# Attention scores as three float32r products in two 64-row halves of the array, in place of six bf16 products over 96 rows

## The chip, the cores and the metric

The kernel runs on one core of a Trainium2 chip. The metric is the device time of one execution in microseconds (us). Engines: PE (TensorE, matmuls), DVE (VectorE), ACT (ScalarE), POOL (GpSimd), SP (SyncE, which issues most DMAs). PEld is PE's weight load.

## What is computed

```python
xn = layernorm(x)                               # x: [4, 2048, 256] float32
q, k, v = xn @ wq.T, xn @ wk.T, xn @ wv.T       # 16 heads of 16; 4 groups share a k and a v head
att = softmax(causal(q k^T / 4)); attn = (att v) @ wo.T
# soft mixture of 16 experts with 64 slots each
y = layernorm(xn) * norm_g + norm_b
logits = y . layernorm(slot_embeds); dispatch = softmax over tokens; combine = softmax over slots
slots = dispatch^T y; eout = (gelu(slots Wg + bg) * (slots Wu + bu)) Wd + bd
out = x + attn + combine eout
```

All is computed to about float32 accuracy, so products are made of parts: a float32 number is split into several numbers of a narrower type, and the products of the parts are summed.

## The kernel before

The stages run one after another, each a block with an instruction stream per engine and semaphores between them: prepare, project, attend, dispatch, experts, combine.

`project` goes over 16 chunks of 512 tokens. DVE takes layer-norm statistics (L303, L306) and normalises x and then xn (L319, giving xn and y), POOL makes the reciprocal roots (L351, L353), PE transposes and makes q, k and v (L450; `pj` has three PSUM banks of q, q and v|k), ACT copies. q and k are split into three bf16 parts: ACT casts `pj` to part 0 (L407), DVE subtracts it to `rest` (L327), ACT casts `rest` to part 1 (L413), POOL subtracts to part 2 (L361, `thirds`). SP writes the parts, y, y transposed and v to DRAM.

`attend` works per batch (4) and group (4): `qs` holds the parts of q stacked in 6 x 16 = 96 rows, `ks` those of k, in the orders `Q_PART` and `K_PART`, so that one matmul over 96 rows sums six products of parts. Two more rows (97 and 98) hold minus the row maximum (`mrow`, as two bf16 parts) in `qs` and ones in `ks`. A group has 40 units: (c, kb) are 512 queries and 128 keys. In a step PE makes

- four s products (L768) of the unit into `sT`, for four heads, in two pairs, each pair followed by an exp on ACT (L642, 128 x 1024), which POOL masks on the diagonal (L624);
- four x products (L726): the same scores the other way around, for 128 queries and up to 512 keys, 20 steps ahead (`LEAD`), into three PSUM banks `mb` (`NBANK`). DVE takes their maxima, with L666 below the diagonal and the masked L671 of 128 to 512 columns on it. `MAXES` gives their order;
- the V product (L751) of the step before: four heads into four 32-column strips of the array, plain float32, eight instructions.

`entries` puts the x products in the step: one after each pair of s, one or more after, V, and one last. At the end of each c DVE makes nm and nml (L701 to L706), PE transposes (L731), DVE copies to `mrow` (L685), and SP writes the row to `qs` (L601). The context goes out by L737, L690, L693 and L604. Twenty steps of x alone lead in (250 to 300 us in the trace). `load(b, g)` on SP fetches a group (13 DMAs, L585 to L587); the four first loads come at the start, later ones when a group is done. PE is one in-order stream: the code lets it wait for DVE's bank, for ACT's exp and for the loads in turn.

Of the kernel before, what the change touches and what calls it, by code (L numbers as in the profile page):

```python
# [23 lines left out]
P = 128  # L24
# [16 lines left out]
Q_PART = (0, 0, 1, 1, 0, 2)  # L41
K_PART = (0, 1, 0, 1, 2, 0)
KR = HD * len(Q_PART)
VW = 32
# [26 lines left out]
def prepare(nc, w, io):  # L71
    with ExitStack() as ctx:
# [12 lines left out]
        ident, identb = w["ident"], w["identb"]  # L85
# [20 lines left out]
        with nc.Block() as block:  # L106
# [21 lines left out]
            def _(pool):  # L128
# [7 lines left out]
                pool.wait_ge(zeroed, 3)  # L136
# [3 lines left out]
                pool.wait_ge(made, 1)  # L140
                nc.gpsimd.tensor_copy(identb[:], ident[:]).then_inc(made, 1)
                pool.wait_ge(step, 2 * SB)
                nc.gpsimd.tensor_scalar(rs[:], mv[:, :, 1], EPS, None, ALU.add).then_inc(made, 1)
                pool.wait_ge(made, 4)
# [3 lines left out]
            def _(dve):  # L148
# [27 lines left out]
                for i, (parts, dest, _) in enumerate(jobs):  # L176
                    dve.wait_ge(turned, i + 1)
                    src = bank[:, i % 8, 0:dest.shape[1]]
                    if i == 0:
                        for k in range(DK):  # L180
                            ins = nc.vector.tensor_copy(
                                w["wqT"][:, k, :].rearrange("p (g d h) -> p g h d", g=NKV, h=GS),
                                bank[:, 0, k * D:(k + 1) * D].rearrange("p (g h d) -> p g h d", g=NKV, h=GS))
# [11 lines left out]
            def _(pe):  # L195
                pe.wait_ge(made, 3)
# [12 lines left out]
def project(nc, w, io, scr):  # L209

    with ExitStack() as ctx:
# [9 lines left out]
        part = a.sb("part", [P, 2, 3, 3, CH], BF16)  # L221
        rest = a.sb("rest", [P, 3, CH])
# [14 lines left out]
        pj_ready, p1_ready, rest_ready, p2_ready, p3_ready = (  # L237
            sem(n) for n in ("pj_ready", "p1_ready", "rest_ready", "p2_ready", "p3_ready"))
# [4 lines left out]
        credits = [(xn_ready, 2 * TPC), (xT_kept, DK), (yT_kept, DK), (rest_ready, 3),  # L243
                   (p3_ready, 3), (v_ready, 1), (vp_ready, 1), (out[0], 16 * NOUT), (out[1], 16 * NOUT),
# [16 lines left out]
        with nc.Block() as block:  # L261
            @block.sync
            def _(sp):
# [5 lines left out]
                def chunk(i, j, q):  # L269
                    sp.wait_ge(y_ready, i * TPC + TPC)  # L270
                    sp.dma_start(scr["y"][i], y[:, q]).then_inc(out[q], 16)
                    wait_apart(sp, p3_ready, 3 * i + 6, passed)
                    for m in range(2):
                        sp.dma_start(scr["q_out"][i, m], part[:, q, m]).then_inc(out[q], 16)
                    sp.dma_start(scr["k_out"][i], part[64:128, q, 2]).then_inc(out[q], 16)
# [12 lines left out]
            def _(dve):  # L288
# [186 lines left out]
def attend(nc, w, scr):  # L475
# [19 lines left out]
    with ExitStack() as ctx:  # L495
# [80 lines left out]
        with nc.Block() as block:  # L576
            @block.sync
            def _(sp):
# [11 lines left out]
                for g in range(NKV):  # L590
                    load(0, g)
# [899 lines left out]
```

## Time and profile before

| | |
|---|---|
| median of 3 runs | 3144.43 us (3142.61 to 3147.72) |
| profiled execution, span from first to last instruction | 3140.2 us |
| profiled execution's own time outside its span | not shown |
| PE / PEld / DVE / ACT / POOL busy | 2696.9 / 1453.6 / 2430.9 / 1627.3 / 622.6 us |
| granted TensorE clock, mean | 0.946 of 2.4 GHz |

A group of instructions is given by line, engine, operation, `out<-in`, and shape as partitions x elements. "Idle before" names what ended the wait. Busy time counts overlapping instructions once, and a matmul's length has its latency in it: the pace of a stream is read from starts.

### The profile page before, as it was taken

The numbers are of one execution on the slowest core, as the hardware profiler recorded it, in microseconds if no ns is written. First come the engines' busy times: TensorE is split into PE (matmuls) and PEld (weight loads), VectorE is DVE, ScalarE is ACT, GpSimd is POOL, SyncE is SP. The second block draws the span as 40 slices with busy tenths as digits, with TensorE's granted clock in tenths as the row PEclk, the third lists the DMA queues.
The fourth block names the chain that finished last, engine by engine and source line by source line (L and its number), as shares of the span: only waits on it lengthen the run. The fifth ranks groups of instructions, "written<-read, shape, count | busy, mean of one in ns | idle before, by whom it ended". The sixth has DMA issues, their size and how long they took to land. (4 is left out here: it accounts for less than half of the span.)

```text
span 3140.2 us, 58475 instructions
## 1 busy us (share of the span) xinstructions
PE 2696.9 (86%) x17059; PEld 1453.6 (46%) x17059; DVE 2430.9 (77%) x5354; ACT 1627.3 (52%) x2185; POOL 622.6 (20%) x574
## 2 busy tenths in 40 slices
PE   4766999998999998999999999985776866879999
PEld 2431333332333332333333333345675756879999
DVE  6976888887888887888888888747677875755666
ACT  2650666665666665666666666665555652112222
POOL 2540011010010000001000000145254533532000
PEclk8985999998999998999999999998998988989999
DMA  3778022022022202202202000031413314656564
GB/s 121 248 240 106 7 35 35 5 36 34 5 37 35 26 15 35 29 11 35 35 14 28 6 7 5 8 124 66 161 29 145 107 54 154 196 164 221 192 194 151
DMA packets 191631, 247.75 MB, mean 79 GB/s; under 512 B 69892, under 2 KB 146824, under 8 KB 191400
## 3 DMA queue, kind: packets, MB, share of 16 engines
q1 hardware_dynamic: 170632, 224.99, 28.2%
q10 hardware_dynamic: 20768, 19.93, 1.9%
q8 instruction: 115, 1.88, 0.3%
q14 instruction: 116, 0.95, 0.1%
HBM read 148.87 MB, written 95.45 MB: 78 GB/s over the span
## 5 line engine op out<-in xcount | busy, mean ns | idle before, releaser
L642 ACT ACTIVATE att_pr<-att_sT 128x1024 f32<-128x1024 f32 (+3 forms) x1280 | 1080.8, 895 | 709.4 <-PE att_sT L768 708.5
L666 DVE TENSOR_REDUCE att_mx<-att_mb 128x1 f32<-128x512 f32 x1536 | 1000.6, 686 | 65.6 <-PE att_mb L726 44.9
L726 PE MATMUL att_mb<-att_ks,att_qs 96*128 96x512 bf16 (+3 forms) x2560 | 831.3, 360 | 68.7 <-DMA att_v<-v_rows 33.7
L768 PE MATMUL att_sT<-att_qs,att_ks 98*128 98x512 bf16 (+3 forms) x2560 | 680.6, 350 | 22.5 <-issue 11.4
L671 DVE CUSTOM_DVE_ANT_0 att_junk<-att_mb,w_causal 128x128 bf16<-128x128 f32 (+3 forms) x1024 | 491.6, 488 | 187.6 <-PE att_mb L726 131.8
L726 PEld LDWEIGHTS att_mb<-att_ks,att_qs 96*128 96x128 bf16 x2560 | 248.1, 97 | 777.6 <-DVE att_mx L666 318.5
L751 PE MATMUL att_acc<-att_pr,att_v 128*32 128x512 f32 (+3 forms) x5120 | 604.3, 544 | 3.8 <-POOL att_pr L624 1.8
L624 POOL TENSOR_SCALAR_AFFINE_SELECT att_pr<-att_pr 128x512 f32<-128x512 f32 x256 | 162.4, 635 | 1681.8 <-ACT att_pr L642 1681.8
L768 PEld LDWEIGHTS att_sT<-att_qs,att_ks 98*128 98x128 bf16 x2560 | 244.7, 99 | 212.2 <-issue 29.1
L1310 ACT CAST com_e1h<-com_tp 128x1024 fp32r<-128x1024 f32 x64 | 64.5, 1014 | 262.6 <-PE com_tp L1383 236.4
L928 DVE TENSOR_TENSOR dis_dl<-dis_lg,dis_dh 128x512 fp32r<-128x512 f32 x128 | 149.8, 1193 | 59.5 <-ACT dis_dh L894 58.6
L751 PEld LDWEIGHTS att_acc<-att_pr,att_v 128*32 128x32 f32 x5120 | 102.3, 108 | 183.2 <-issue 165.9
L1036 PE MATMUL dis_lp<-dis_yh,dis_dh 128*128 128x258 f32 x256 | 78.2, 306 | 106.6 <-DVE dis_dl L928 106.6
L1401 PE MATMUL com_mp<-com_eoh,com_e1h 128*128 x512 | 146.3, 286 | 7.9 <-DVE com_e1l L1335 7.9
L1401 PE MATMUL com_mp<-com_eol,com_e1h 128*128 x512 | 145.9, 285 | 0.0
L1401 PE MATMUL com_mp<-com_eoh,com_e1l 128*128 x512 | 145.8, 285 | 0.0
L894 ACT CAST dis_dh<-dis_lg 128x512 fp32r<-128x512 f32 x128 | 79.0, 617 | 89.6 <-PE dis_dp L1036 49.4
L888 ACT ACTIVATE dis_lg<-dis_lg 128x512 f32<-128x512 f32 x128 | 79.8, 627 | 70.8 <-POOL dis_lg L996 70.8
L1011 PE MATMUL dis_lp<-w_seTh,dis_yTh 128*128 128x512 f32 x256 | 102.3, 400 | 12.6 <-POOL dis_yTl L977 11.7
L996 POOL TENSOR_TENSOR dis_lg<-dis_lg,dis_ca 128x512 f32<-128x512 f32 x64 | 100.2, 1598 | 56.9 <-issue 56.9
L1036 PEld LDWEIGHTS dis_lp<-dis_yh,dis_dh 128*128 128x128 f32 x256 | 51.6, 202 | 112.0 <-DVE dis_dl L928 112.0
L1401 PEld LDWEIGHTS com_mp<-com_eoh,com_e1h 128*128 128x128 f32 x512 | 99.3, 194 | 8.7 <-issue 8.7
(170 smaller groups left out, 4051.4 us busy)
## 6 DMA issues: line engine op xcount, KB each, us to landing
slot_exps<-dis_e SPq DMA_DIRECT2D x64, 512.0 KB, 2.7
com_e<-slot_exps SPq DMA_DIRECT2D x64, 512.0 KB, 3.5
att_qs<-q_parts SPq DMA_DIRECT2D x96, 256.0 KB, 9.7
q_parts<-proj_part SPq DMA_DIRECT2D x32, 384.0 KB, 3.3
y_rows<-proj_y SPq DMA_DIRECT2D x16, 512.0 KB, 4.6
y_cols<-proj_yT SPq DMA_DIRECT2D x16, 512.0 KB, 4.6
context<-att_cn SPq DMA_DIRECT2D x64, 128.0 KB, 2.0
dis_yT<-y_cols SPq DMA_DIRECT2D x16, 512.0 KB, 3.5
```

The lines of the kernel that those rows point to most:

```text
L624: nc.gpsimd.affine_select(out=blk, in_=blk, compare_op=ALU.is_ge, fill=0.0, base=0, pattern=[[0, GS], [1, P]], channel_multiplier=-1).then ...
L642: nc.scalar.activation(pr[:, s % 4, 2 * hf:2 * hf + 2, off:CH], sT[:, 2 * hf:2 * hf + 2, off:CH], ACT.Exp, scale=float(HD) ** -0.5).then_i ...
L666: nc.vector.tensor_reduce(dst, mb[:, bank, :], AX.X, ALU.max).then_inc(mb_used, 1)
L671: nc.vector.tensor_tensor_reduce(junk[:, t % 2, 0:wd], mb[:, bank, 0:wd], w["causal"][:, CH - wd:CH], 1.0, LOW, ALU.add, ALU.max, dst).the ...
L726: last = nc.tensor.matmul(mb[:, bank, 0:wd], qs[0:KR, g % NKV, c, q0:q0 + P], ks[0:KR, g % NKV, j * CH:j * CH + wd], start=True, stop=True)
L751: last = nc.tensor.matmul(acc[VW * h:VW * (h + 1), off:CH], v[:, g, kb, :], pr[:, s % 4, h, off:CH], start=(kb == 0), stop=(kb == TPC * (c ...
L768: last = nc.tensor.matmul(sT[:, h, off:CH], ks[:, g, kb * P:(kb + 1) * P], qs[:, g, c, h * CH + off:(h + 1) * CH], start=True, stop=True)
L928: nc.vector.tensor_tensor(dl[:, m % ND], lg[:, t, hf * 512:(hf + 1) * 512], dh[:, m % ND].bitcast(F32), ALU.subtract).then_inc(dl_ready, 1)
L996: nc.gpsimd.tensor_tensor(lg[:, t, h], lg[:, t, h], ca[:, h], ALU.subtract).then_inc(sub_p, 1)
L1011: last = nc.tensor.matmul(lp[:, 2 * (t % 2) + h, :], lhs[:, t // TPC, k, (t % TPC) * P:(t % TPC + 1) * P], w[rhs][:, k, h * 512:(h + 1) * ...
L1036: last = nc.tensor.matmul(bank(hf * HB + s)[:, 0:D + 2], lhs[:, (hf * TPB + t) % ND, s * P:(s + 1) * P], rhs[:, t, :], start=(t == 0 and l ...
L1401: last = nc.tensor.matmul(mp[:, q, 0:D], lhs[:, q, s, :], rhs[:, b, s, :], start=(s == 0 and rhs is eoh and lhs is e1h), stop=(s == SB - 1 ...
```

## The change

q and k are split into two float32r parts (no second cast on ACT, no thirds on POOL, no `rest`), and three products of parts are summed: 48 rows in place of 96. `qs` and `ks` are float32r and hold two copies side by side: rows 0 to 49 for two of the four heads, rows 64 to 113 for the other two (k is loaded twice). The x and s products of one head then use only the upper or lower 64 rows of the array. The order of `MAXES` has the head innermost, so that successive x products alternate the halves; within a step all four x now have the same t and j. The rows of ones come by DMA, and PE waits for them first. V, ACT's exps, the kinds and number of DVE's maxima and all later stages are as before.

```diff
-Q_PART = (0, 0, 1, 1, 0, 2)
-K_PART = (0, 1, 0, 1, 2, 0)
+Q_PART = (0, 0, 1)
+K_PART = (0, 1, 0)
 KR = HD * len(Q_PART)
+RG = 64
+NRG = P // RG
+HL = GS // NRG
...
-        part = a.sb("part", [P, 2, 3, 3, CH], BF16)
-        rest = a.sb("rest", [P, 3, CH])
+        part = a.sb("part", [P, 2, 3, 2, CH], F32R)
...
                 def splits(i, q):
                     for s in range(3):
-                        dve.wait_ge(p1_ready, 3 * i + s + 1)
-                        dve.wait_ge(p3_ready, 3 * i + s + 1)
+                        dve.wait_ge(high_ready, 3 * i + s + 1)
                         r = rows(s)
-                        nc.vector.tensor_tensor(rest[r, s, :], pj[r, s, :], part[r, q, s, 0, :],
-                                                ALU.subtract).then_inc(rest_ready, 1)
+                        nc.vector.tensor_tensor(part[r, q, s, 1, :], pj[r, s, :], part[r, q, s, 0, :].bitcast(F32),
+                                                ALU.subtract).then_inc(low_ready, 1)
...
-                def thirds(i, q):
-                    for s in range(3):
-                        pool.wait_ge(p2_ready, 3 * i + s + 1)
-                        pool.wait_ge(p3_ready, 3 * i + s + 3)
-                        r = rows(s)
-                        nc.gpsimd.tensor_tensor(part[r, q, s, 2, :], rest[r, s, :], part[r, q, s, 1, :],
-                                                ALU.subtract).then_inc(p3_ready, 1)
...
-                    for s in range(3):
-                        r = rows(s)
-                        act.wait_ge(rest_ready, 3 * i + 3 + s + 1)
-                        nc.scalar.copy(part[r, q, s, 1, :], rest[r, s, :]).then_inc(p2_ready, 1)
...
-    MAXES = [(c, h, t, j) for c in range(CPB) for h in range(GS) for t in range(TPC) for j in range(c + 1)]
+    MAXES = [(c, h, t, j) for c in range(CPB) for t in range(TPC) for j in range(c + 1) for h in range(GS)]
...
-        qs = a.sb("qs", [KR + 2, NKV, CPB, GS * CH], BF16)
-        ks = a.sb("ks", [KR + 2, NKV, S], BF16)
+        qs = a.sb("qs", [RG + KR + 2, NKV, CPB, HL * CH], F32R)
+        ks = a.sb("ks", [RG + KR + 2, NKV, S], F32R)
...
                 def load(b, g):
-                    for j in range(len(Q_PART)):
-                        r = slice(HD * j, HD * (j + 1))
-                        sp.dma_start(qs[r, g], scr["q_in"][b, Q_PART[j], g]).then_inc(loaded[g], 16)
-                        sp.dma_start(ks[r, g], scr["k_in"][b, K_PART[j], g]).then_inc(loaded[g], 16)
+                    for rg in range(NRG):
+                        for j in range(len(Q_PART)):
+                            r = slice(RG * rg + HD * j, RG * rg + HD * (j + 1))
+                            sp.dma_start(qs[r, g].bitcast(F32), scr["q_in"][b, Q_PART[j], g, rg]).then_inc(loaded[g], 16)
+                            sp.dma_start(ks[r, g].bitcast(F32), scr["k_in"][b, K_PART[j], g]).then_inc(loaded[g], 16)
...
-                for g in range(NKV):
+                load(0, 0)
+                for rg in range(NRG):
+                    for hl in range(2):
+                        row = RG * rg + KR + hl
+                        sp.dma_start(ks[row:row + 1].rearrange("o g s -> o (g s)").bitcast(F32),
+                                     w["ones"][:].bitcast(F32)).then_inc(ones_set, 16)
+                for g in range(1, NKV):
                     load(0, g)
...
-                nc.vector.memset(ks[KR:KR + 2, :, :], 1.0).then_inc(ones_set, 1)
...
-                            for hl in range(2):
-                                sp.dma_start(qs[KR + hl:KR + hl + 1, g % NKV, c, :],
-                                             mrow[hl * ROWS:(hl + 1) * ROWS, c, :]).then_inc(m_rows[c], 16)
+                            for rg in range(NRG):
+                                row = RG * rg + KR
+                                sp.dma_start(qs[row:row + 2, g % NKV, c, :].bitcast(F32),
+                                             mrow[rg * ROWS:(rg + 1) * ROWS, c, :].bitcast(F32)).then_inc(m_rows[c], 16)
...
-                            q0 = h * CH + t * P
+                            r = slice(RG * (h % NRG), RG * (h % NRG) + KR)
+                            q0 = h // NRG * CH + t * P
                             wd = CH if j < c else (t + 1) * P
-                            last = nc.tensor.matmul(mb[:, bank, 0:wd], qs[0:KR, g % NKV, c, q0:q0 + P],
-                                                    ks[0:KR, g % NKV, j * CH:j * CH + wd], start=True, stop=True)
+                            last = nc.tensor.matmul(mb[:, bank, 0:wd], qs[r, g % NKV, c, q0:q0 + P],
+                                                    ks[r, g % NKV, j * CH:j * CH + wd], start=True, stop=True)
...
-                            for h in (2 * hf, 2 * hf + 1):
-                                last = nc.tensor.matmul(sT[:, h, off:CH], ks[:, g, kb * P:(kb + 1) * P],
-                                                        qs[:, g, c, h * CH + off:(h + 1) * CH], start=True, stop=True)
+                            for rg in ((0, 1), (1, 0))[hf]:
+                                r = slice(RG * rg, RG * rg + KR + 2)
+                                last = nc.tensor.matmul(sT[:, NRG * hf + rg, off:CH], ks[r, g, kb * P:(kb + 1) * P],
+                                                        qs[r, g, c, hf * CH + off:(hf + 1) * CH], start=True, stop=True)
```

`q_out` and `k_out` write two float32 parts in place of three bf16 ones; nml and mrow are float32r (32 x 128 float32 is transposed and copied), in an order by halves; the four copies of wq transposed in prepare put the heads by halves.

## Rows read from the trace of the kernel before

**Rows 1.** The page's first line

```profile
span 3140.2 us, 58475 instructions
```

**Rows 2.** Windows: stretch, length, busy us (instructions) by engine, clock, DMA share, GB/s

```profile
120.00:150.00 30.00, 23.34 (x93) 13.34 (x94) 28.64 (x72) 18.50 (x33) 18.02 (x21) 0.94 0.83 267
250.00:300.00 50.00, 36.97 (x82) 8.52 (x82) 42.01 (x130) 0.00 (x0) 0.00 (x0) 0.50 1.07 128
524.30:633.30 109.00, 103.43 (x662) 35.49 (x661) 94.84 (x250) 69.27 (x85) 10.15 (x16) 1.00 0.20 27
```

**Rows 3.** Groups by shape, DVE, one group of attention (866.4 to 975.3)

```profile
L693 DVE TENSOR_TENSOR att_cn<-att_mb,att_rz 128x256 f32<-128x256 f32 x4 | 1.7, 424 | 0.2
L690 DVE RECIPROCAL att_rz<-att_mb 128x16 f32<-128x16 f32 x4 | 1.0, 258 | 0.3 <-DVE att_mx L666 0.2
L685 DVE COPY att_mrow<-att_mb 32x128 bf16<-32x128 bf16 x4 | 0.8, 204 | 0.0
```

**Rows 4.** Timeline of PE, one step: start us, length us, what

```profile
1006.73 0.23 PE L726 MATMUL att_mb<-att_ks,att_qs 96*128 96x128 bf16 x1
...
1007.90 0.60 PE L726 MATMUL att_mb<-att_ks,att_qs 96*128 96x512 bf16 x2
1008.43 1.07 PE L751 MATMUL att_acc<-att_pr,att_v 128*32 128x512 f32 x8
1009.43 0.28 PE L726 MATMUL att_mb<-att_ks,att_qs 96*128 96x256 bf16 x1
```

**Rows 5.** Timeline of DVE in attention, masked and full maxima

```profile
922.49 0.29 DVE L671 CUSTOM_DVE_ANT_0 att_junk<-att_mb,w_causal 128x128 bf16<-128x128 f32 x1
...
922.78 0.42 DVE L671 CUSTOM_DVE_ANT_0 att_junk<-att_mb,w_causal 128x256 bf16<-128x256 f32 x1
...
923.14 0.56 DVE L671 CUSTOM_DVE_ANT_0 att_junk<-att_mb,w_causal 128x384 bf16<-128x384 f32 x1
...
1005.29 0.68 DVE L671 CUSTOM_DVE_ANT_0 att_junk<-att_mb,w_causal 128x512 bf16<-128x512 f32 x1
...
1005.90 1.88 DVE L666 TENSOR_REDUCE att_mx<-att_mb 128x1 f32<-128x512 f32 x3
1007.70 0.28 DVE L671 CUSTOM_DVE_ANT_0 att_junk<-att_mb,w_causal 128x128 bf16<-128x128 f32 x1
```

**Rows 6.** Timelines of PE, dispatch and combine: float32r products back to back

```profile
2250.42 0.39 PE L1011 MATMUL dis_lp<-w_seTl,dis_yTh 128*128 128x512 f32 x1
2250.65 0.40 PE L1011 MATMUL dis_lp<-w_seTh,dis_yTl 128*128 128x512 f32 x1
...
2900.05 0.19 PEld L1401 LDWEIGHTS com_mp<-com_eol,com_e1h 128*128 128x128 f32 x1
2900.17 0.19 PEld L1401 LDWEIGHTS com_mp<-com_eoh,com_e1l 128*128 128x128 f32 x1
```

**Rows 7.** Timelines in projection: PE, POOL, DVE and SP

```profile
122.10 0.65 SPq L271 DMA_DIRECT2D y_rows<-proj_y  x1
...
124.94 3.62 POOL L361 TENSOR_TENSOR proj_part<-proj_rest,proj_part 128x512 bf16<-128x512 f32 x3
...
125.48 3.56 DVE L319 TENSOR_SCALAR proj_y<-proj_xn,proj_mv,proj_rs 128x256 f32<-128x256 f32 x4
...
130.87 1.38 DVE L319 TENSOR_SCALAR proj_xn<-proj_x,proj_mv,proj_rs 128x256 f32<-128x256 f32 x4
...
139.76 1.88 PE L450 MATMUL proj_pj<-proj_xT,w_wkvT 128*128 128x512 f32 x4
...
144.00 0.65 SPq L271 DMA_DIRECT2D y_rows<-proj_y  x1
```

**Rows 8.** Loads: PE's and SP's timelines

```profile
301.82 0.61 PE L768 MATMUL att_sT<-att_qs,att_ks 98*128 98x512 bf16 x1 [8.68 <-DMA att_qs<-att_mrow]
...
415.52 0.38 SPq L585 DMA_DIRECT2D att_qs<-q_parts  x1
...
421.82 0.39 SPq L587 DMA_DIRECT2D att_v<-v_rows  x1
```

More of the change, by code:

```diff
@@ L135, in _ @@
                 nc.gpsimd.memset(w["causal"][:], 0.0).then_inc(zeroed, 1)
-                pool.wait_ge(zeroed, 3)
+                nc.gpsimd.memset(w["ones"][:].bitcast(F32), 1.0).then_inc(zeroed, 1)
+                pool.wait_ge(zeroed, 4)
                 tri = w["causal"][:, CH - P:CH]
@@ L180, in _ @@
                         for k in range(DK):
-                            ins = nc.vector.tensor_copy(
-                                w["wqT"][:, k, :].rearrange("p (g d h) -> p g h d", g=NKV, h=GS),
-                                bank[:, 0, k * D:(k + 1) * D].rearrange("p (g h d) -> p g h d", g=NKV, h=GS))
+                            for r in range(NRG):
+                                ins = nc.vector.tensor_copy(
+                                    w["wqT"][:, k, :].rearrange("p (g d r e) -> p r g e d", g=NKV, d=HD, r=NRG)[:, r],
+                                    bank[:, 0, k * D:(k + 1) * D].rearrange("p (g e r d) -> p r g e d", g=NKV, r=NRG,
+                                                                            d=HD)[:, r])
                         ins.then_inc(kept, 1)
@@ L271, in chunk @@
                     sp.dma_start(scr["y"][i], y[:, q]).then_inc(out[q], 16)
[L272 removed]
+                    wait_apart(sp, low_ready, 3 * i + 6, passed)
                     for m in range(2):
[L274 to L275 removed]
+                        sp.dma_start(scr["q_out"][i, m], part[:, q, m].bitcast(F32)).then_inc(out[q], 16)
+                    sp.dma_start(scr["k_out"][i], part[64:128, q, 2].bitcast(F32)).then_inc(out[q], 16)
                     sp.wait_ge(yT_kept, DK * i + 2 * DK)
@@ L369, in step @@
                         roots(1, i + 1, 1 - q)
-                    thirds(i, q)
                 roots(0, 0, 0)
@@ L504, in attend @@
         nm = a.sb("nm", [P, ROWS])
-        nml = a.sb("nml", [P, 2, ROWS], BF16)
-        mrow = a.sb("mrow", [2 * ROWS, CPB, P], BF16)
+        nml = a.sb("nml", [P, NRG, 2, HL * TPC], F32R)
+        mrow = a.sb("mrow", [2 * ROWS, CPB, P], F32R)
         cT = a.sb("cT", [P, 2, CH])
@@ L730, in fill @@
                             pe.wait_ge(nm_ready, b * NMC + g * CPB + c + 1)
-                            last = nc.tensor.transpose(mb[0:2 * ROWS, bank, 0:P // 2].bitcast(BF16),
-                                                       nml[:, :, :].rearrange("p a r -> p (a r)"), w["identb"][:])
+                            last = nc.tensor.transpose(mb[0:2 * ROWS, bank, 0:P],
+                                                       nml[:].rearrange("p r a x -> p (r a x)").bitcast(F32),
+                                                       w["ident"][:])
                         else:
```

46 lines of the change are left out of this document (21 added, 25 removed).

## The prediction

> **What bounds the kernel now.** I read the page first, then windows by stage, then the groups of one steady stretch, and last timelines of single steps. The windows split the 3140.2 us span [rows 1]: weights and projection until 230, a lead-in of row maxima from 250 to 300, attention from 301.8 to about 2068, and then dispatch, experts and combine, which the change does not touch. Attention is 56% of the span and repeats every 109 us, one group of 40 steps (4 batches x 4 groups = 16 groups). In such a group PE is busy 103.4 us and DVE 94.8 [rows 2].
>
> A step holds four score products for the maxima (x, L726), four transposed score products (s, L768), eight value matmuls (V, L751) and, on DVE, four maxima. The starts on PE in one full step [rows 4] show what paces it: from 1006.73 (a 128-wide x) through 4 s and 3 x of 512 columns to the V at 1008.43 is 1.70 us, and from there to the next x at 1009.43 is 1.00. A bf16 product of 512 columns thus takes 0.22 us, and a full step 8 x 0.216 + 1.00 = 2.73 us, which is 109/40. DVE needs 0.60 us per full maximum by its starts (1005.90 to 1007.70 is three [rows 5]), 2.40 per full step. So in attention PE is the bound and DVE is close behind. ACT, 69 us per group, is not near.
>
> The lead-in is DVE and DMA: it begins when the first load has landed (250.5) and PE's first s waits until 301.8 for a DMA [rows 8], behind the loads of all four groups, at 128 GB/s with the DMA engines full [rows 2]. Projection repeats every 10.9 us (y_rows issued at 122.10 and, two chunks on, at 144.00 [rows 7]) with DVE busy 95% and DMA share 0.83 at 267 GB/s [rows 2].
>
> **The change, part by part.**
>
> *Score products, PE.* K falls from 96 or 98 rows to 48 or 50, placed in rows 0-63 or 64-127 of the array; the order of x and s now alternates the halves (0 and 1): s0 s1, x0 of half 0, s1 s0, x1 of half 1, x2 of half 0, V, x3 of half 1. If two halves run at once, a pair takes the time of one. A float32r product of 512 columns starts every 0.233 us (2250.42 to 2250.65) and one of 256 every 0.12 [rows 6], so a pair should take 0.233, or 0.117 each; the weight load of 0.188 us is seen to hide at a pitch of 0.12 in the 256-column rows. I take 0.12 each whatever the width: 8 x 0.12 = 0.96, and a full step on PE becomes 1.96 us in place of 2.73. No row shows two row halves at work. The nearest is V: four heads in four column strips, 8 matmuls in 1.00 us [rows 4], where plain float32 instructions of 512 columns over the whole array start every 0.43 us (four in 1.88, the last one's 0.59 taken off), 3.4 for eight [rows 7]. Strips do run at once there. Bounds: 0.117 per product (full overlap) and 0.233 (none). I take overlap. The Trainium skill ("TensorE: Matmul & The Clock Gate", Part 3) says that matmuls in different row groups run concurrently, four of 32 rows giving 3.07x; by that two halves would give at least 1.5x. No run here shows it yet. The skill's "TensorEngine Tiling", Key Properties, speaks against: changing the tiling mode drains the engine. Both kernels change mode twice a step around V, and the trace has about 0.1 us there (1007.90 + 2 x 0.22 = 1008.33, V at 1008.43), which is in my 1.00 and stays.
>
> *Who is the bound then.* DVE. Its maxima keep their kinds and number: per group 96 full at 0.60 and 16 each of the masked ones of 512, 384, 256 and 128 columns at 0.61, some 0.48 (between its neighbours), 0.36 and 0.29 (starts 1005.29 to .90, 922.78 to 923.14, 922.49 to .78 [rows 5]). The new order of MAXES puts four of one kind in a step: 24 steps of 4 x 0.60 = 2.40, 4 of 2.44, and 12 whose DVE work (1.92, 1.44, 1.16) is under PE's 1.96, so PE sets those. Sum of the larger: 57.6 + 9.8 + 23.5 = 90.9; nm, nml, mrow, rz and cn on DVE add 4 x (0.8 + 0.7) = 6 (0.42 for cn, four small ones of some 0.2 for nm, nml and mrow, one of 0.26 for rz [rows 3]). That is 97. Frictions: x2 must wait for its bank (three banks), then V sits in front of x3. A waiting x issues at 0.03, a float32r product lands some 0.5 later, V begins at 0.45, x3 issues at 1.45 and lands at 1.95, where DVE wants it at 1.80: 0.15 x 24 = 3.6. Group: 100.5, against 108.9. Bounds: 96.5 (no friction), and 105 if the frictions stay what they are now (PE's own work sums to 97 per group: 139,264 columns at 2.4 per ns are 58, V 35, transposes and gaps 4; the larger of PE and DVE step by step to 102; measured 109, so 6.7), with 128-wide float32r products slower than I assume. 301.8 to the last maximum is 15.5 groups: 15.5 x 8.4 = **130 us** gained (60 to 190). The last 20 steps have no maxima; ACT (1.94 per full step) and V pace them: 0. The instruction fetch between batches: unchanged.
>
> *Row of maxima.* nml, the transpose and mrow go to float32r: 4 each per group, 0.2 us each, the DMA of each half is 512 B per piece in place of 256: 0. The memset on DVE (6.88 us, in an idle stretch) is replaced by four 32 KB DMAs into single rows; PE's first instruction now waits for them behind load 0. Their 131 KB would take 1 us at the 128 GB/s of the loads; in 256-byte pieces into one row each I take 4, bounds 1 and 10.
>
> *Loads.* Each group's load goes from 13 to 25 DMAs, 0.47 us of SP each (415.52 to 421.82 is 12 steps; 11.7 us, was 6) [rows 8], and from 2.23 to 2.62 MB (q 1.57 MB either way, k 0.39 to 0.79). At 128 GB/s the four first loads take 82 us in place of 70: **+12**, and +4 for the ones. In mid-run a load takes 17 to 20 us at that rate, then 20 to 23. What queues behind it on SP and the rings is the row of maxima for c=2, issued 11.6 us after the load begins; it is due when step 12 of the group starts, 12 x 2.5 = 30 us. It would land at about 25: hidden, with 5 us to spare. Nothing else on SP is due before.
>
> *Projection.* Gone: ACT's second cast (3 x 0.62 per chunk), POOL's thirds (3.62). DVE's subtraction stays and writes the low part. The gain comes from elsewhere: DVE's four norms of y take 3.56 us while POOL runs the thirds, and the same form on x takes 1.38 when POOL is idle [rows 7]. With POOL quiet DVE's chunk is 10.9 - 2.2 = 8.7 us. The Trainium skill ("SBUF — State Buffer", the shared port pair of DVE and GpSimd, held for a whole instruction) gives the reason; the trace agrees, 0.89 against 0.35 us. But DMA grows: q_out 384 to 512 KB, k 192 to 256, 2752 to 3072 KB a chunk, 3.15 MB at 267/0.83 = 322 GB/s full rate = 9.8 us; the fastest window shows more, so 9.5. Gain 1.4 x 15 = 21, taken as **20 us**, plus 2 at the tail; bounds 0 and 33.
>
> So the first s moves from 301.8 by -22 + 12 + 4 = -6 us (-25 to +12). Sum: -130 - 6 = -136. The span is 3140.2 and the median of the runs 3144.4, the 4 us between them I leave; 3144.4 - 136 = **3008 us**.
>
> **Rivals.**
> 1. *The halves don't overlap.* Then each product costs 0.233 in place of 0.216, narrow ones 0.12 in place of 0.06: 5.4 + about 1 us per group on PE, which remains the bound, and the full/masked bunching on DVE (3.1 us steps beside short PE steps) adds 2. For: no row shows halves. Against: the column strips of V. 15.5 x 6 to 8 = +93 to 125, less 6: about **3240**, slower. The point from which it decides is a pitch of about 0.18 us per product: 8 x 0.18 + 1.0 = 2.44 is DVE's step; above 0.21 the kernel is slower.
> 2. *Overlap, but the step is held near its old length* by the chain x2-V-x3 and three banks, or by narrow products: group 105 to 109, time **3060 to 3140**. For: DVE idles 14 us per group now, most on x of PE. Against: PE would have 20% slack that it has not now.
> 3. *The clock.* PE is granted 2.4 GHz in attention (1.00), but 0.50, its 1.2 GHz level, throughout the lead-in, where it is busy 37 of 50 us, and 0.94 in projection at 23.3 of 30 [rows 2]. After the change PE idles a fifth of the step. At the low level a full step costs 1.7 + 2.0 = 3.7 us, 1.3 over DVE's. If an eighth of the 1560 us falls low, that is about 70 us back: **3080**. Against: the gaps would be under 0.5 us, where projection has gaps of 3 us and keeps 0.94.
> 4. *The load is late*: if a load takes over 29 us, the c=2 row stalls s in each of 12 groups; 5 us each, +60, **3070**. The rate of the first loads speaks against.
>
> **How the numbers follow.** Mine 0.60 (own range 2955 to 3080), rival 1 0.18, rival 2 0.10, rival 3 0.08, rival 4 0.04. The last three lie mostly between 3060 and 3135. The range is 2950 to 3130, which leaves out rival 1 and little more. The bound of what a measurement tells from no change is 0.2%, 6 us. Faster 0.79, same 0.02, slower 0.19.
>
> **What would show it.** In the profile after: s and x starts in pairs a few ns apart or 0.12 us apart on average, and not 0.23; loads of a group issued every 101 us, not 109; DVE busy over 92% of a group and PE under 85%; DVE's y norms at 0.35 us; first s near 296. A PE step of over 2.7 us with x and s at 0.23 makes rival 1 right, a granted clock under 0.95 in attention rival 3, a wait of s for mrow at kb = 0 rival 4.

## The result and the profile after

The changed kernel takes 3294.06 us (median of 4 runs, 3275.83 to 3306.62), the kernel before 3143.56 (3142.61 to 3147.72): ratio 1.0468, interval 1.0435 to 1.0501. It is slower by 150 us, where 136 us of gain were predicted. The profiled execution takes 3285.96 us. Now and then an execution of a kernel is slower at a lower clock; the ratios below leave these out. The first line of the page of the kernel after, and its windows (columns as in [rows 2]):

```profile
span 3284.2 us, 58210 instructions
```

```profile
120.00:150.00 30.00, 25.99 (x100) 14.87 (x99) 24.89 (x81) 15.52 (x29) 7.76 (x12) 0.94 0.93 318
250.00:300.00 50.00, 32.83 (x63) 17.07 (x63) 34.12 (x92) 0.00 (x0) 0.00 (x0) 0.50 1.05 127
340.00:1900.00 1560.00, 1439.95 (x8563) 627.63 (x8564) 1222.09 (x3220) 899.10 (x1090) 131.96 (x208) 0.85 0.20 26
1000.00:1120.00 120.00, 112.71 (x656) 49.41 (x653) 94.15 (x246) 68.61 (x84) 10.15 (x16) 0.82 0.22 28
1188.00:1192.00 4.00, 3.92 (x30) 1.69 (x23) 3.45 (x10) 2.46 (x4) 0.00 (x0) 1.00 0.00 0
1192.00:1196.00 4.00, 2.78 (x21) 1.43 (x18) 2.53 (x15) 2.12 (x3) 0.63 (x1) 0.90 0.01 2
1196.00:1200.00 4.00, 4.00 (x20) 1.59 (x17) 2.18 (x11) 2.23 (x4) 0.63 (x1) 0.50 0.01 2
1204.00:1208.00 4.00, 3.48 (x17) 1.54 (x9) 2.97 (x11) 1.94 (x2) 0.00 (x0) 0.50 0.00 0
1212.00:1216.00 4.00, 4.00 (x20) 2.27 (x20) 2.42 (x6) 1.94 (x2) 0.00 (x0) 0.50 0.01 2
1220.00:1224.00 4.00, 3.97 (x28) 1.61 (x23) 3.10 (x9) 3.00 (x4) 0.00 (x0) 1.00 0.02 4
```

The same window of the kernel before:

```profile
340.00:1900.00 1560.00, 1461.78 (x9256) 499.67 (x9248) 1332.13 (x3477) 972.79 (x1179) 142.13 (x224) 0.99 0.17 24
```

Attention is where the time went: the last s product starts at 2204.4 us, where it was 2063.8. The granted clock of the window from 340 to 1900 was 0.99, and is 0.85 now. Cut into windows of 5 us, 23% of that stretch are below 0.60, most of them at 0.50, the 1.2 GHz level. The last six rows follow one such episode: the clock is 1.00; PE is then busy for only 2.78 of 4 us; the clock falls, and at 1220 it is back. In between PE is busy nearly all the time (3.48 of 4 us in one window, 4.00 in the others), so a busy PE alone did not bring it back at once.

What stands before the fall is the end of a c: PE waits for the last maxima and for nml before it can transpose the row of maxima. The transpose in the kernel after (in the episode above), and one in the kernel before:

```profile
1193.80 0.28 PE L726 MATMUL att_mb<-w_ident,att_nml 128*32 128x128 f32 x1 [0.83 <-DVE att_mx L664]
```

```profile
931.06 0.23 PE L731 MATMUL att_mb<-w_identb,att_nml 128*32 128x128 bf16 x1 [0.88 <-DVE att_mx L666]
```

In windows of 1 us from 303 to 1900 the clock falls to 0.50 35 times, and 23 of these falls come within 5 us behind such a transpose. The kernel before has the same waits (at this transpose PE waits 129 us in all 64 cases together, 118 us in the kernel after), yet its clock falls only 5 times, and never behind a transpose. So the wait is where the clock falls, but it is not new; what is new is the lighter work around it (experiments 1, 10 and 11). Group loads are issued like this in SP's timeline, 120 us apart where the group before took 109:

```profile
1020.65 0.39 SPq L575 DMA_DIRECT2D att_v<-v_rows  x1
...
1140.92 0.39 SPq L575 DMA_DIRECT2D att_v<-v_rows  x1
```

One full step at full clock in PE's timeline, and a step at the lower level:

```profile
1107.52 1.07 PE L747 MATMUL att_acc<-att_pr,att_v 128*32 128x512 f32 x8
1108.52 0.49 PE L721 MATMUL att_mb<-att_ks,att_qs 48*128 48x512 f32 x1
1108.52 0.72 PE L765 MATMUL att_sT<-att_qs,att_ks 50*128 50x512 f32 x2
1108.86 0.39 PE L721 MATMUL att_mb<-att_ks,att_qs 48*128 48x512 f32 x1
1109.09 0.40 PE L765 MATMUL att_sT<-att_qs,att_ks 50*128 50x512 f32 x2
1109.32 0.97 PE L721 MATMUL att_mb<-att_ks,att_qs 48*128 48x512 f32 x2
1110.22 1.06 PE L747 MATMUL att_acc<-att_pr,att_v 128*32 128x512 f32 x8
...
1266.39 1.94 PE L747 MATMUL att_acc<-att_pr,att_v 128*32 128x512 f32 x8
1268.26 0.79 PE L721 MATMUL att_mb<-att_ks,att_qs 48*128 48x512 f32 x1
```

The same step on DVE, and on PE's weight loads:

```profile
1109.05 0.69 DVE L659 TENSOR_REDUCE att_mx<-att_mb 128x1 f32<-128x512 f32 x1 [0.21 <-PE att_mb L721]
```

```profile
1109.79 0.18 PEld L721 LDWEIGHTS att_mb<-att_ks,att_qs 48*128 48x128 f32 x1 [0.52 <-DVE att_mx L659]
```

The halves do run at once: x and s start together at 1108.52, and the next two products 0.34 later. The step is still 2.70 us, because of a loop: V (1107.52 to 1108.52, 1.00), x3 behind it lands, which is the time from its start until DVE begins (0.53), the maximum (0.61), its bank comes free for x2 of the next step, which waits for it (0.13), and V starts 0.43 after that x. The sum is 2.70. At 1.2 GHz V alone takes 1.87 (1266.39 to 1268.26).

Before attention the chunk period of projection is now 9.4 to 10.6 us (SP's y_rows issues at 123.23, 132.65 and 143.25), against 10.9 [rows 7], and DVE's norms of y have come down from 3.56 us:

```profile
127.34 1.38 DVE L321 TENSOR_SCALAR proj_y<-proj_xn,proj_mv,proj_rs 128x256 f32<-128x256 f32 x4
130.15 1.41 DVE L305 BATCH_NORM_STATS2 proj_st<-proj_x 128x6 f32<-128x256 f32 x4 [1.42 <-DMA proj_x<-in_L_attn_x_dram]
```

DVE now waits for DMA there. The first load is issued at 211.46 us, 18.5 earlier than before. PE's first x and first s in its timeline:

```profile
240.31 0.69 PE L721 MATMUL att_mb<-att_ks,att_qs 48*128 48x128 f32 x3 [40.00 <-DMA att_ks<-w_ones]
...
300.70 0.80 PE L765 MATMUL att_sT<-att_qs,att_ks 50*128 50x512 f32 x2 [16.28 <-DMA att_qs<-att_mrow]
```

The first s is at 300.70, against 301.82 [rows 8]: the earlier start is eaten by the longer loads.

### The profile page after: what moved, and what is told of

Read it like the earlier page. It is cut to its first block and busy times, and to the rows that moved or that the text cites. A ratio compares the mean times of both kernels' runs of the same rounds, so it can differ in the third digit from the quotient of the medians.

```text
span 3284.2 us, 58210 instructions
## 1 busy us (share of the span) xinstructions
PE 2807.6 (85%) x17059; PEld 1668.5 (51%) x17059; DVE 2385.8 (73%) x5355; ACT 1599.6 (49%) x2137; POOL 561.7 (17%) x526
## 5 line engine op out<-in xcount | busy, mean ns | idle before, releaser
L721 PE MATMUL att_mb<-att_ks,att_qs 48*128 48x512 f32 (+3 forms) x2560 | 1034.3, 474 | 114.8 <-DMA att_ks<-w_ones 40.0
L659 DVE TENSOR_REDUCE att_mx<-att_mb 128x1 f32<-128x512 f32 x1536 | 971.6, 684 | 164.3 <-PE att_mb L721 162.3
L721 PEld LDWEIGHTS att_mb<-att_ks,att_qs 48*128 48x128 f32 x2560 | 500.0, 214 | 893.3 <-DVE att_mx L659 463.5
L747 PE MATMUL att_acc<-att_pr,att_v 128*32 128x512 f32 (+3 forms) x5120 | 698.0, 622 | 1.8 <-ACT att_pr L637 1.0
L765 PE MATMUL att_sT<-att_qs,att_ks 50*128 50x512 f32 (+3 forms) x2560 | 669.7, 445 | 30.7 <-DMA att_qs<-att_mrow 16.3
L664 DVE CUSTOM_DVE_ANT_0 att_junk<-att_mb,w_causal 128x128 bf16<-128x128 f32 (+3 forms) x1024 | 467.5, 488 | 273.2 <-issue 176.1
L765 PEld LDWEIGHTS att_sT<-att_qs,att_ks 50*128 50x128 f32 x2560 | 364.0, 215 | 76.6 <-issue 32.2
L1033 PE MATMUL dis_lp<-dis_yh,dis_dh 128*128 128x258 f32 x256 | 78.3, 306 | 107.5 <-DVE dis_dl L925 107.5
```

The costliest lines, as they stand in the source:

```text
L659: nc.vector.tensor_reduce(dst, mb[:, bank, :], AX.X, ALU.max).then_inc(mb_used, 1)
L664: nc.vector.tensor_tensor_reduce(junk[:, h % 2, 0:wd], mb[:, bank, 0:wd], w["causal"][:, CH - wd:CH], 1.0, LOW, ALU.add, ALU.max, dst).the ...
L721: last = nc.tensor.matmul(mb[:, bank, 0:wd], qs[r, g % NKV, c, q0:q0 + P], ks[r, g % NKV, j * CH:j * CH + wd], start=True, stop=True)
L747: last = nc.tensor.matmul(acc[VW * h:VW * (h + 1), off:CH], v[:, g, kb, :], pr[:, s % 4, h, off:CH], start=(kb == 0), stop=(kb == TPC * (c ...
L765: last = nc.tensor.matmul(sT[:, NRG * hf + rg, off:CH], ks[r, g, kb * P:(kb + 1) * P], qs[r, g, c, hf * CH + off:(hf + 1) * CH], start=Tru ...
L1033: last = nc.tensor.matmul(bank(hf * HB + s)[:, 0:D + 2], lhs[:, (hf * TPB + t) % ND, s * P:(s + 1) * P], rhs[:, t, :], start=(t == 0 and l ...
```

## The experiments

All times are medians. The ratio is to the kernel before, run beside each, with its 95% interval; where there is none, the lowest and highest time stand instead. The clock is the granted clock of the profiled execution in the window 340 to 1900.

| kernel | us | ratio and interval | clock |
|---|---|---|---|
| changed kernel | 3294.06 | 1.0468 (1.0435 to 1.0501) | 0.85 |
| 1 s doubled | 3148.61 | 1.0006 (0.9995 to 1.0018) | 0.97 |
| 2 full rows | 3264.35 | 1.0375 (1.0352 to 1.0398) | 0.99 |
| 3 old order | 3493.18 | 1.1084 (1.1048 to 1.1121) | 0.75 |
| 4 V in bf16 | 3214.86 | 1.0220 (1.0196 to 1.0244) | 0.50 |
| 5 V in bf16, s tripled | 3177.34 | 3136.34 to 3193.06 us | 0.87 |
| 6 two x behind V | 3160.32 | 1.0040 (1.0026 to 1.0053) | 0.97 |
| 7 the same, half doubled | 3185.73 | 1.0146 (1.0115 to 1.0176) | 0.93 |
| 8 V cut in two | 3975.17 | 1.2562 (1.2502 to 1.2623) | 0.55 |
| 9 the same, half doubled | 3932.29 | 1.2335 (1.2271 to 1.2399) | 0.65 |
| 10 before, 48 rows | 3973.65 | 3907.91 to 4005.70 us | 0.59 |
| 11 62 rows per half | 3195.78 | 1.0187 (1.0144 to 1.0229) | 0.95 |
| 12 before, V in bf16 | 2933.53 | 0.9330 (0.9312 to 0.9349) | 0.95 |
| 13 the same, 126 rows | 2886.65 | 0.9204 (0.9172 to 0.9236) | 0.98 |
| 14 before, 126 rows | 3142.51 | 0.9996 (0.9985 to 1.0008) | 0.99 |
| 15 ones late | 3286.11 | 1.0462 (1.0431 to 1.0493) | 0.84 |

**1. More work on PE, nothing else.** Each s product is issued twice.

```diff
-                            for rg in ((0, 1), (1, 0))[hf]:
+                            for rg in 2 * ((0, 1), (1, 0))[hf]:
```

> The changed kernel with each s product issued twice into the same place (the result is the same), so that PE has 0.94 us more columns to do in a full step, 0.47 us if the halves overlap. Clock theory: the changed kernel lost its time because PE, with half the columns to stream, idles between products and is granted 1.2 GHz in about 31% of attention (mean 0.847), where a full step takes 3.8 us in place of 2.7. More work should bring the clock in attention back to 0.97 or more and the time down by about 0.27 x 1910 x 0.29 = 150 us, to 3110-3160 us. Loop theory: a full step at the full clock stays at 2.7 us, since V, x3, its maximum, x2 and the next V wait for one another and the doubled products lie in PE's slack. Rival (PE's work decides, the halves hardly overlap): clock unchanged or up a little, steps longer, time at or above 3290 us.

Measured: 3148.61 us, so 145 of the 150 us lost are gone though PE does more. It is again the time of the kernel before (ratio 1.0006). Groups take 107.5 to 110.8 us.

```profile
340.00:1900.00 1560.00, 1483.12 (x11452) 800.32 (x11446) 1323.68 (x3465) 968.95 (x1172) 142.31 (x224) 0.97 0.20 27
```

So the low clock is what made the changed kernel slower than the one before. Full steps are still 2.6 to 2.7 us: the gain that was predicted is absent at full clock too.

**2. No halves.** x and s use rows from 0 to 111 or 113, so that products run one after another; the rows between are zeroed and the output sums two heads.

```diff
-                                r = slice(RG * rg, RG * rg + KR + 2)
+                                r = slice(0, RG + KR + 2)
```

> The changed kernel with each x and s product taken over all 112 or 114 rows at once (both halves, so the scores of two heads are added: the output is another), and the rows between the halves set to 0. The rest is as in the changed kernel. Nothing can overlap: a product of 512 columns should start every 0.233 us, PE's full step is 8 x 0.233 + 1.0 = 2.87 us. Clock theory: PE has no idle time left, the clock in attention is 0.97 or more, steps 2.9 us, and although PE does twice the streaming the time is below the changed kernel's: 3200-3250 us. Rival (the clock has another cause, such as float32r or the halves themselves being slow): clock stays near 0.85 and the time rises above 3350 us.

Measured: 3264.35 us, groups of 114.9 to 115.6, full steps of 2.9 to 3.1. This is the price of rival 1, 6 us a group; and yet it is faster than the changed kernel, since the clock stays up. Part of the excess over the expectation is the zeroing, which puts the first s at 325.46.

**3. The old order of MAXES**, so that x products mostly stay in one half.

```diff
-    MAXES = [(c, h, t, j) for c in range(CPB) for t in range(TPC) for j in range(c + 1) for h in range(GS)]
+    MAXES = [(c, h, t, j) for c in range(CPB) for h in range(GS) for t in range(TPC) for j in range(c + 1)]
```

> The changed kernel with the order of MAXES as before the change (head outermost), so that a step has full and masked maxima mixed, and successive x products are mostly of one half. Bunching theory (four masked maxima in a step leave DVE and PE waiting in turn): a group gets up to 5 us shorter, time 3200-3250 us. Clock and loop theory: the x products overlap less with their neighbours and the idle gaps are spread more evenly, the full-clock step stays 2.6-2.7, the clock is a little higher, time 3230-3300 us. If alternation in x matters much: above 3300 us.

Measured: 3493.18 us, the last case of the expectation (above 3300), and far above it. 46% of the 5 us windows are below 0.60; at full clock the steps are 2.5 to 2.9. Bunching maxima of one kind is not what costs. That the alternation of the halves is what helped fits this, but the order changes the mix of maxima too, so it is not shown alone.

**4 and 5. V in bf16**, alone and with s tripled: four V instructions in place of eight.

```diff
-        pr = a.sb("pr", [P, 4, GS, CH])
+        pr = a.sb("pr", [P, 4, GS, CH], BF16)
```

(`v` and `v_rows` likewise; in 5 also `for rg in 3 * ...`.)

> The changed kernel with the exps and v in bf16, so that V is four products of one pass in place of eight instructions of float32 (the low parts of the probabilities and of v are left out). V falls from 1.0 us to about 0.3 in a full step. Loop theory: the loop V, x3, maximum, x2, V falls from 2.7 to 2.0 us, so DVE becomes the bound with 2.4-2.5 us per full step, a group near 98-101 us. Clock theory: PE's activity falls further, the granted clock goes below 0.8, perhaps to 0.5-0.6, but even at 1.2 GHz PE's step is 8 x 0.21 + 0.5 = 2.2 us and DVE stays the bound: time 2990-3050 us. Rival (steps held by something else, the bunched maxima or ACT): groups stay above 108 us and the time above 3150 us.

> The run with V in bf16 (the low parts of the probabilities and of v are left out; 3214.86 us, clock 0.50 in the whole of attention) with each s product issued three times. PE's work per full step at full clock is 8 x 0.12 for the first copies, 8 x 0.12 for the others and some 0.3 for V, 2.2 us. Clock theory: active for 2.2 of 2.4 us, so the clock comes back to 2.4 GHz for at least nine tenths of attention. Loop theory: with V at 0.3 the loop is under 2.1 us, so DVE's 2.4 is the bound: full steps of 2.4 to 2.5, groups of 99 to 102, time 2990 to 3060. If the clock stays at 0.50 in spite of the copies, PE at 1.2 GHz has 4.4 us of work per step, and the time is over 3600.

Measured in 4: 3214.86 us with the clock at 0.50 in every window of attention; the size was missed, since at 1.2 GHz V, landing, maximum and x still make 2.5 to 2.9. In 5 the copies bring the clock back for most of the time, and the loop shows. PE's timeline:

```profile
512.55 0.40 PE L747 MATMUL att_acc<-att_pr,att_v 128*32 128x512 bf16 x4
512.88 0.50 PE L721 MATMUL att_mb<-att_ks,att_qs 48*128 48x512 f32 x1
...
515.00 0.40 PE L747 MATMUL att_acc<-att_pr,att_v 128*32 128x512 bf16 x4
```

DVE's timeline of the same step:

```profile
512.63 4.29 DVE L659 TENSOR_REDUCE att_mx<-att_mb 128x1 f32<-128x512 f32 x7 [0.21 <-PE att_mb L721]
```

V holds PE for 0.33 and not 1.00, the step is 2.45, and DVE runs seven maxima without a gap: the bound that the prediction had named appears once V is short. The time (expected 2990 to 3060) was missed because 21% of the windows are still below 0.60, and with three copies a step at the low level takes up to 5.3 us.

**6 and 7. Two x behind V** (s doubled; then only the first pair).

```diff
-                    tail = min(1, sum(e[0] == "x" for e in todo))
+                    tail = min(2, sum(e[0] == "x" for e in todo))
```

> The change with the s products issued twice (as in the run with doubled s, 3148.61 us, groups of 107.5 to 110.8 us), and V moved ahead of the last two x products in place of the last one. Loop theory: with one x behind V the full step is V, x3 landing, its maximum, x2, V, 2.70 us. With V ahead of x2 and x3, V waits only for x1, DVE has two maxima (1.2 us) to do while V runs (1.0), and the bound becomes PE's own work, 1.96 + 0.5 for the second copies = 2.46 us, near DVE's 2.4. Full steps of 2.45 to 2.55, groups of 103 to 105, the clock as in the doubled run (0.977), time 3060 to 3110. If the step was held by something else (the second copies themselves, or ACT), nothing changes: 3140 to 3155, steps at 2.7.

> As the run before it (V ahead of the last two x), but only the first pair of s of each step is issued twice: PE's own work is 2.21 us per full step, under DVE's 2.4. Loop theory with the clock kept: full steps of 2.42 to 2.5, groups of 101 to 103, time 3030 to 3070. Clock theory: PE is active for 2.21 of about 2.45 us, 0.90, where the doubled run had 2.46 of 2.7, 0.91, and the changed kernel 1.96 of 2.7, 0.73; so the mean granted clock in attention should stay over 0.95. If it falls under 0.9 the extra pair was needed, and the time is 3100 to 3200.

Measured: 3160.32 and 3185.73 us; my reading of the loop was wrong in its place. PE in 6:

```profile
609.56 1.06 PE L747 MATMUL att_acc<-att_pr,att_v 128*32 128x512 f32 x8
610.56 0.50 PE L721 MATMUL att_mb<-att_ks,att_qs 48*128 48x512 f32 x2
...
611.83 0.49 PE L721 MATMUL att_mb<-att_ks,att_qs 48*128 48x512 f32 x1
612.25 1.06 PE L747 MATMUL att_acc<-att_pr,att_v 128*32 128x512 f32 x8
```

DVE in 6:

```profile
611.09 1.29 DVE L659 TENSOR_REDUCE att_mx<-att_mb 128x1 f32<-128x512 f32 x2 [0.33 <-PE att_mb L721]
```

The step is 2.69 again, with the same terms: V 1.00, landing 0.53, maximum and release 0.74, x to V 0.42. With four x a step and three banks, the x three places behind the first one after V is always the last before the next V, wherever V stands. Run 7, with fewer copies, has the lower clock (0.93), and was expected to keep it over 0.95.

**8 and 9. V cut into two column halves**, around x2 (9: first pair of s doubled).

```diff
+                    if main and 1 <= s <= STEPS:
+                        values(b, s - 1, 0)
+                    fill(b, s, limit, rest)
                     if main and 1 <= s <= STEPS:
-                        values(b, s - 1)
+                        values(b, s - 1, 1)
```

> The changed kernel with the V product cut into two halves of the columns, one ahead of x2 and one between x2 and x3 (all float32, nothing left out, no doubled products). Loop theory: three banks tie each x behind V to the x three places later, which stands ahead of the next V; wherever V stands, the loop is V (1.0), landing (0.52), maximum (0.61 and 0.1 to the release), x, V (0.43), 2.70 us, which is why moving V ahead of two x left the steps at 2.7. Cut in half, V stands in each loop with 0.5, and the loop is 2.2. Then PE's own work, 0.96 + 1.0 + two more changes of strips of 0.2 each, and DVE's 2.4 decide: warm full steps of 2.4 to 2.55, and PE is active for nearly all of the step, so the clock should be above the changed kernel's 0.85. Time 3050 to 3150. If the loop is not it, warm steps stay at 2.7 or grow by the changes of strips to 2.9.

> The run with V cut in two, and the first pair of s of each step issued twice (0.25 us more PE work per full step, which holds the clock up if activity is what it goes by). Loop theory with the clock kept: PE's own work 2.6 to 2.65 per full step, groups of 104 to 107, time 3080 to 3140. If the clock without the second copies is at 0.97 or more already, this run is slower than the one with V cut in two alone by up to 50 us; if that one is at 0.9 or less, this one is faster.

Contrary to what the first of these expects, part of the context sum changes: both halves begin with `start` in one bank, and what the first 128 keys add to the first half of the columns is most likely lost. The Trainium skill ("PSUM — Partial Sum Buffer", The four PSUM rules) has it that a second group begun in the same bank and quadrant makes the first one's next product overwrite; no run here shows this by itself. Every product is still made. Measured: 3975.17 and 3932.29 us. In a full-clock stretch of 8 no x waits for DVE, and the step is 2.70 by PE alone:

```profile
613.20 0.64 PE L749 MATMUL att_acc<-att_pr,att_v 128*32 128x256 f32 x8
613.77 0.49 PE L721 MATMUL att_mb<-att_ks,att_qs 48*128 48x512 f32 x1
614.19 0.64 PE L749 MATMUL att_acc<-att_pr,att_v 128*32 128x256 f32 x8
614.76 0.49 PE L721 MATMUL att_mb<-att_ks,att_qs 48*128 48x512 f32 x1
...
615.90 0.42 PE L749 MATMUL att_acc<-att_pr,att_v 128*32 128x256 f32 x4
```

A lone x between two V pieces occupies 0.42 of PE where a pair of halves takes 0.23 to 0.34. The clock fell to 0.55, with PE busy for 1538 of the 1560 us of the window; why it fell this far is not shown. The run doesn't test the loop either, as PE's own work fills the step.

**10. The number of rows, in the kernel before.** Three bf16 products of parts over 48 rows in place of six over 96.

```diff
-Q_PART = (0, 0, 1, 1, 0, 2)
-K_PART = (0, 1, 0, 1, 2, 0)
+Q_PART = (0, 0, 1)
+K_PART = (0, 1, 0)
```

> The kernel before the change with three bf16 products over 48 rows in place of six over 96 (the three smallest products of parts are left out); each matmul has the same columns and the same duration, only half of the rows of the array. Theory A, the clock follows the time for which PE streams: nothing changes, granted clock 0.98 and more in attention, groups of 108 to 110, time 3125 to 3145 (the loads are smaller). Theory B, the clock follows how much of the array is at work: x and s have half the rows as in the changed kernel, and the clock falls in attention as there, to 0.9 or lower, and the time is 3200 or more.

```profile
340.00:1900.00 1560.00, 1531.68 (x6092) 427.54 (x6091) 906.73 (x2292) 670.41 (x774) 93.39 (x147) 0.59 0.08 11
```

The matmuls, their columns and their order are the same (only the loads are smaller), and the time is 3973.65 us, 830 us more (765 by the fastest execution): that is what half the rows cost. Once the clock has fallen it stays low for long: four of the seven falls from 303 to 1900 last 204 to 307 us each, with PE busy for 98% of the window. So it is not idle time that keeps the clock at 0.59, and as nothing else on PE was changed, it is how much of the array is at work.

**11. The number of rows, in the changed kernel.** Each half is filled with zero rows: 62 for x, 64 for s, the maxima and ones moved to rows 62 and 63 (`MR`).

```diff
-                            r = slice(RG * (h % NRG), RG * (h % NRG) + KR)
+                            r = slice(RG * (h % NRG), RG * (h % NRG) + MR)
...
-                                r = slice(RG * rg, RG * rg + KR + 2)
+                                r = slice(RG * rg, RG * rg + RG)
```

> The changed kernel with each half filled up: rows 48 to 61 of each half hold zeros, the row maximum and the ones stand in rows 62 and 63; x uses 62 rows of a half in place of 48, s 64 in place of 50. Instructions, columns, number type and results are those of the changed kernel; the zeros are written once, ahead of the first load (some 30 to 50 us, once). If the granted clock follows the rows at work, it rises in attention from 0.85 towards the 0.98 of the doubled run, the share of stretches at 0.5 falls from 24% to under 10%, groups go from 113 to 126 us to 109 to 113, and the attention takes 1790 to 1850 us in place of 1910; with the delay of the first load the time is 3190 to 3270. If the rows don't matter (zeros, or only how long products stream), groups stay at 113 to 126 and the time is 3320 or more.

```profile
340.00:1900.00 1560.00, 1413.32 (x9172) 612.79 (x9172) 1301.59 (x3446) 963.72 (x1167) 139.06 (x219) 0.95 0.20 27
```

Measured: 3195.78 us, 98 less than the changed kernel, although the zeroing puts the first s at 334.33, 34 us later. Fourteen rows of zeros per half took the low windows from 23% to 4%. The clock still falls 26 times, 23 of them behind a transpose of the maxima, but 22 of the falls last only 3 to 4 us; in the changed kernel half of them last 13 us or more. So here the rows did not so much prevent the falls as end them sooner.

**12, 13 and 14. The kernel before with V in bf16**, then with x over 126 and s over 128 rows (30 of zeros), then those rows at full precision.

> The kernel before the change with V in bf16 (the low parts of the probabilities and of v are left out). PE's work per full step falls from 2.73 to 8 x 0.216 + 0.3 = 2.03 us with no row halves in it. If the clock follows how much of the step PE is active, whatever the halves, it falls as in the changed kernel (2.03 of 2.4, 0.85, against its 0.73 at 0.85 mean clock): some windows low, mean clock 0.85 to 0.98, time 3030 to 3120. If the fall has to do with work in halves of the array, the clock stays at 0.98 and more, DVE's 2.4 is the bound, and the time is 3000 to 3030.

> The kernel before the change with V in bf16 (the low parts of the probabilities and of v are left out; 2933.53 us, clock 0.945 in attention), with x and s over 126 and 128 rows in place of 96 and 98, the added rows zero. If the clock follows the rows, its low stretches (8% of attention) go, and with them about 130 us x 0.5 of step time at most where PE sets the pace at 1.2 GHz: groups from 95.5 to 92 to 94, time 2890 to 2925. If it does not, 2930 to 2945, the delay of the first x by the longer fill with it.

> The kernel before, nothing left out, with x and s over 126 and 128 rows in place of 96 and 98, the added rows zero. In attention its granted clock is 0.99 already, 2% of its stretches at 0.5, so the rows can give back at most 1560 x 0.01 to 0.02 x (share of the step that PE sets) = 5 to 20 us: 3120 to 3140, groups of 108 to 109 as before. If the extra rows cost anything (later first x), 3145 to 3150.

Measured: 2933.53, 2886.65 and 3142.51 us. 12 and 13 leave out the low parts of V's factors, so they show where the bound lies and are no replacement for the kernel. Windows of 13, and its DVE in one steady stretch:

```profile
340.00:1900.00 1560.00, 1370.70 (x7926) 557.41 (x7925) 1428.07 (x3786) 1124.87 (x1367) 201.22 (x273) 0.98 0.20 32
```

```profile
604.20 1.88 DVE L670 TENSOR_REDUCE att_mx<-att_mb 128x1 f32<-128x512 f32 x3
605.99 0.68 DVE L675 CUSTOM_DVE_ANT_0 att_junk<-att_mb,w_causal 128x512 bf16<-128x512 f32 x1
...
606.60 1.88 DVE L670 TENSOR_REDUCE att_mx<-att_mb 128x1 f32<-128x512 f32 x3
```

DVE has no gap here, groups take 93 us, near the sum of its own work, and attention is DVE's. So it was shortening V, not x and s, that reached DVE's bound. My range for 12 (3000 to 3120 over both theories) was too high: it took 2.4 us for every step, but many steps of that order have a masked maximum among the four and are shorter. Work over 96 rows does not keep the clock up by itself: in 12 it is 0.95, and the filling takes 47 us more off (expected: 2890 to 2925, so a little more than I thought). In 14 there is little low time to win, and nothing is won.

**15. The wait for ones moved to the first s.**

```diff
-                pe.wait_ge(ones_set, 16 * 2 * NRG)
...
+                        if s == 0:
+                            pe.wait_ge(ones_set, 16 * 2 * NRG)
```

> The changed kernel with PE's wait for the rows of ones moved from the start of the lead-in to the first s of each batch. In the changed kernel PE waits 40 us for them, and its first x starts at 240.3, 29 us after the first load is issued, where it was 21 before. If the lead-in's maxima set when attention starts, the first s moves forward by up to 8 us, from 300.7 to 293. If the four loads set it (as my sum had it), the first x moves and the first s stays within 2 us of 300.7. The attention behind it stays at 1910 us, give or take the scatter of the clock (20 us).

Measured: PE's first x at 238.45 in a run whose first load was issued at 212.52, 26 us behind it against 29; the first s at 302.09. The four loads set the start of attention, and the ones cost nothing.

## Why the prediction was wrong, point by point

- **The halves overlap**: right. Pairs start within 0.01 us, at a pitch of 0.23 to 0.34 for two. What the Trainium skill says of row groups ("TensorE: Matmul & The Clock Gate", Part 3), that matmuls in different ones run concurrently, holds in these traces. Rival 1 did not happen; experiment 2 gives its price, 6 us a group, as worked out.
- **"Who is the bound then. DVE"**: wrong, and the first step that failed. The term that was mis-sized is the friction, "0.15 x 24 = 3.6". Its pieces make a loop of 2.55 us, and the loop measures 2.70: the release of the bank to x2 takes 0.13 and not 0.03, and landing, maximum and x to V 0.03, 0.01 and 0.01 more. Worse, I charged it to the 24 steps of full maxima alone and let the 12 narrow ones run at PE's 1.96. The loop holds those too: with the maxima of [rows 5] in place of 0.61 it would be 2.57, 2.45 and 2.38 us. Single steps don't follow this, but pairs do: a step of 2.70 and a narrow one should take 5.27, 5.15 and 5.08 us, and the two steps that share a narrow set take 5.29, 5.18 and 5.11 in a group of experiment 1. So 28 x 2.70 + 4 x (2.57 + 2.45 + 2.38) = 105.2 us is an estimate of the steps, 10.7 over the forecast's (3.6 for the 24 full ones, 1.0 for the four masked ones of 512 columns, 6.1 for the 12 narrow ones). It leaves out that V is shorter on the diagonal and that steps with a transpose are longer (3.0 to 4.0 us); the groups of experiment 1 come to 107.5 to 110.8 us, not 100.5. Of the 130 us of gain in attention nothing came. Rival 2 described this, at chance 0.10.
- **The clock** (rival 3, chance 0.08): right in mechanism, mis-sized, and the second step that failed. "If an eighth falls low", 70 us: a mean of 0.85 means that 30% is at the low level, and its cost is 3294.06 - 3148.61 = 145 us, or a little more, as the clock of experiment 1 is 0.97 and not 0.99. My argument against it looked at the length of gaps, as projection has longer ones. Experiments 10 and 11 show that rows count, and the term for them was missing.
- **Together**: 130 of gain absent and 145 of clock make 275 of the 286 us between 3008 and 3294; 5 more are the first s (296 expected, 300.70 seen).
- **Projection and loads**: right in kind. The norms of y are 1.38 us as forecast, the first load came 18.5 us earlier (22 forecast), and from it to the first s are 89.2 us, 17.3 more than before (16 forecast). The ones took no time that counts (experiment 15).
- **Rival 4**: the load is not late. The costliest groups of the page after show s waiting 16.3 us for mrow in all, and that is the first s:

```profile
L765 PE MATMUL att_sT<-att_qs,att_ks 50*128 50x512 f32 (+3 forms) x2560 | 669.7, 445 | 30.7 <-DMA att_qs<-att_mrow 16.3
```


What stays open: why float32r products over 48 rows in halves keep a mean clock of 0.85, and bf16 products over 48 rows one at a time only 0.59. Number type, overlap and order all differ there. Open too is why cutting V in two brought 0.55.

## What to carry to other kernels

Before making an engine's part of a step shorter, follow the loop through its buffers: add up every term from one long instruction to the next that depends on it through a bank, the start of the last product before it included. A faster TensorE step that uses less of the array can cost the clock, so read the granted clock in the stage that is changed. If it fell, test with doubled products, or with zero rows: these made no step longer here, cost 34 us of zeroing once, and recovered 98 of the 150 us lost. Shorten the instruction that the loop runs through (V here), not the one that has the most busy time.

## What the runs showed of the hardware

- The granted clock follows how much of the array works, not only whether PE is busy: 96 to 48 rows at the same instructions took it from 0.99 to 0.59 with PE busy 98%; 48 to 62 rows per half took it from 0.85 to 0.95 with PE busy less (1439.95 to 1413.32 us). Zeros count as rows.
- The same short wait of PE can cost the clock or not: with 0.8 to 0.9 us at the transpose of the maxima the clock fell behind it 23 times in the changed kernel and never in the kernel before.
- Two float32r products in halves of 64 rows start together; a pair takes 0.23 to 0.34 us for 512 columns at the full clock.
- V begins 0.43 us after the start of a 512-column product over half the rows in float32r, of which 0.22 to 0.23 is the product.
